# Six row buffers, earlier token numbers, zeros ahead of the first group, and ScalarE issuing the experts' weight loads in one layer of an eight-layer kernel

## The chip, the cores and the metric

One core of one Trainium2 chip runs one launch of the whole kernel. The metric is the device time of the launch in microseconds (us): the median of the runs shown.

## The reference, cut to what matters

The kernel computes eight residual blocks over 1024 tokens of 256 numbers. Only the fourth, called layer 3 in the kernel, is touched by the change. It is a mixture of experts: 128 experts are scored, 48 of them are kept, each token picks 8, and each expert takes at most 96 tokens.

```python
def _L1_ffn_ref(hidden_states, gate_weight, gate_up_proj, down_proj, old_to_new):
    NUM_EXPERTS = 128; NUM_KEPT = 48; TOP_K = 8; HIDDEN = 256; INTER = 96; CAP = 96
    logits = x @ gate_weight.T
    logits = jnp.where(old_to_new[None, :] == -1, -jnp.inf, logits)
    probs = jax.nn.softmax(logits, axis=-1)
    top_v, top_i = jax.lax.top_k(probs, TOP_K)
    top_v = top_v / jnp.sum(top_v, axis=-1, keepdims=True)
    sel_new = old_to_new[top_i]
    ...
    pos = jnp.sum(jnp.cumsum(oh, axis=0) * oh, axis=-1) - 1      # place of the token in its expert
    valid = pos < CAP
    xb = jnp.zeros((E, CAP + 1, H)).at[flat_e, pos_c].set(x[tok])[:, :CAP]
    gu = jnp.einsum('ech,eoh->eco', xb, gate_up_proj)
    g, u = jnp.split(gu, 2, axis=-1)
    out = jnp.einsum('eci,ehi->ech', jax.nn.silu(g) * u, down_proj)
    y = out[flat_e, jnp.minimum(pos_c, CAP - 1)]
    w = flat_w * valid
    final = jnp.zeros_like(x).at[tok].add(y * w[:, None])
```

## The kernel before

All matrix products split each float32 operand into a high and a low float16 part and sum three products (`mm3`, its matmuls carry line 863).

**Layer 3** takes the 48 experts in 12 groups of four (`QUADS`). The four experts of a group have 384 slots together, which are three chunks of 128 (`CHUNKS`). The work of group q is, engine by engine:

- **Slot numbers.** VectorE writes one-hot matrices (`one_hot`, L1982) that say which token sits in which slot. TensorE multiplies them with a table `wsplit` (`slots`, L1035) that holds each token's weights and, in its last 64 columns, its number (written at L1990). VectorE turns the result into indices (`slot_rows`, L1948 and L1949).
- **Rows.** GpSimd gathers the token rows of each chunk from the scratch table `rows` in HBM with an indirect DMA (L665) into one of `ROW_BUFS` = 4 buffers `x_rows`, all in the tile `sel`. SyncE's queue transposes each chunk into `xe[q % 2]` (`turn_rows`, L584). A gather into a used buffer waits for the transposes of the whole group that used it (L664). The transposes of a group wait until its three gathers have landed (L580) and those of the group before have landed (L582).
- **Weights.** SyncE's queue loads each expert's 320 KB into `w_in[:, j]` (`expert_load`, L569). ScalarE writes the high part (`weights_high`, L1561), VectorE the low part (`weights_low`, L1972). Groups 0 and 1 are loaded far ahead. From group 2 on an expert's load waits until VectorE is done with the buffer's last content (`we_lo`), and in the order of SyncE's queue the loads of group q + 3 stand behind the transposes of group q + 2.
- **Products.** TensorE: `gate_up(q)` (48 matmuls), `slots(q + 2)`, `combine(q - 1)` (48 matmuls of 256 columns into the accumulator, L1072), `down(q)` (L863 again). ScalarE: silu (L1573), high part of the hidden values (L1577), `weights_high(q + 1)`, and the high part of the group's three output chunks (L1587). VectorE: hidden values (L2009), `slot_rows(q + 2)`, low part (L2014), `slot_weights`, `weights_low(q + 1)`, `hot_turned(q)` (L1965), `one_hot(q + 3)`, and the low parts of the three output chunks (L2030).

The third output chunk's high part on ScalarE waits for VectorE's low part of the first. `slots(q + 2)`, which stands behind `gate_up(q + 1)` of the next turn, waits for all three low parts (L1118).

Ahead of group 0 stand, in a row on VectorE, `count_keys` (L1927, L1928, a wait for TensorE's sums, L1931), the token numbers (L1990), and the first `one_hot`. TensorE's queue has `slots(0)`, `turn_weights`, `slots(1)` and `map_weights` (L947, L948) before `gate_up(0)`.

`zeros16` is a tile of zeros; matmuls on it (L1115) clear an accumulator bank. `link` makes VectorE wait for its own last instruction.

Of the kernel before, what the change touches and what calls it, by code (L numbers as in the profile page):

```python
# [20 lines left out]
ALU = mybir.AluOpType  # L21
# [4 lines left out]
P = 128  # L26
D = 256
# [3 lines left out]
NT = T // P  # L31
# [28 lines left out]
KEPT = 48  # L60
# [4 lines left out]
QUAD = 4  # L65
QUADS = KEPT // QUAD
CHUNKS = QUAD * CAP // P
ROW_BUFS = 4
QS = QUAD * CAP
EW = 2 * 2 * INTER3 + D  # L70
# [56 lines left out]
def build(nc, w_blocks, w_experts, w_router, w_attn, x_in, ctxt, tok_ids, mask, g_all, l2_bias_rows, l2_bias_v,  # L127
          l4_gate, o2n_col, o2n_row, k_sel, k_rope, k_ident, k_ident16, k_tri, k_iota, k_slot, k_pick, k_token, k_tokens, out):
    ctx = ExitStack()
    with ctx:  # L130
# [7 lines left out]
        bank = [s2_all[:, i, :] for i in range(6)]  # L138
# [8 lines left out]
        xt_hi = sb("xt_hi", [P, KT, T], F16)  # L147
# [7 lines left out]
        w_in = sb("w_in", [P, RING, 3 * D])  # L155
# [137 lines left out]
        o = 8 * QS  # L293
        x_rows = [sel[:, o + n * 2 * D:o + (n + 1) * 2 * D] for n in range(ROW_BUFS)]
# [189 lines left out]
        def _(sp):  # L484
# [76 lines left out]
            def expert_load(e):  # L561
                j = e % QUAD
                if e >= 2 * QUAD:
                    sp.wait_ge(we_lo, e - 2 * QUAD + 1)
                elif e >= QUAD:
                    sp.wait_ge(we_first, j + 1)
                else:
                    sp.wait_ge(w_split, FFN[1][0] + FFN[1][1])
                sp.dma_start(w_in[:, j, 0:EW], w_experts[e]).then_inc(we_land[j], 16)  # L569
# [27 lines left out]
            for q in range(QUADS):  # L597
                for e in range(QUAD * (q + 2), min(QUAD * (q + 3), KEPT)):
                    expert_load(e)
                if q + 2 < QUADS:  # L600
                    turn_rows(q + 2)
# [255 lines left out]
        def _(pe):  # L857
# [163 lines left out]
            def experts3():  # L1021
# [81 lines left out]
                map_weights()  # L1103
                for q in range(QUADS):
# [357 lines left out]
        def _(act):  # L1462
# [91 lines left out]
            def experts3():  # L1554
# [9 lines left out]
                nc.scalar.activation(silu3[1][0:1, 0:1], ident[0:1, 0:1], ACT.Silu)  # L1564
                act.wait_ge(m_oldt, 3)
# [3 lines left out]
                for q in range(QUADS):  # L1569
# [10 lines left out]
                    for c in range(CHUNKS):  # L1580
# [4 lines left out]
                        if q > 1:  # L1585
                            act.wait_ge(s3_c, q - 1)
                        nc.scalar.activation(y16[q % 2][:, 0, c, :], bank[2 + c % 2][:, (c // 2) * D:(c // 2 + 1) * D],  # L1587
                                             ACT.Copy, scale=w_slot[:, q % 4, c:c + 1]).then_inc(s3_yh, 1)

# [189 lines left out]
        def _(dve):  # L1779
            n_own = [0]  # L1780

            def link(ins):

                n_own[0] += 1
                ins.then_inc(s_v, 1)
                dve.wait_ge(s_v, n_own[0])
# [136 lines left out]
            def count_keys():  # L1923
# [4 lines left out]
                link(nc.vector.tensor_scalar(one3, new, 1.0, None, ALU.min))  # L1928
                dve.wait_ge(m_cum, 1)
# [10 lines left out]
            def experts3():  # L1940
# [48 lines left out]
                for t in range(NT):  # L1989
                    m = nc.vector.tensor_scalar(wsplit[:, t, 2 * 64:3 * 64], zeros16[:, 0:64], token[:, 0:1], float(P * t),  # L1990
                                                ALU.add, ALU.add)
                link(m)
# [613 lines left out]
```

## Time and profile before

| | us |
|---|---|
| median of 3 runs | 1504.42 (1503.94 to 1505.86) |
| the profiled execution | 1502.56 |
| its span, first to last instruction | 1500.7 |
| TensorE busy | 1265.7 (84%) |
| VectorE busy | 1178.3 (79%) |
| GpSimd busy | 762.9 (51%) |
| ScalarE busy | 758.1 (51%) |
| mean granted clock of TensorE | 0.789 of full speed |

The span covers all eight layers; layer 3's part of it lies between about 684 and 871 us. Busy shares are averages over stages with different limits. The granted clock of TensorE is 1.00 (2.4 GHz) or 0.50 (1.2 GHz) at any moment.

### The profile page before, as it was taken

How to read it: one execution, taken by the hardware profiler on the slowest of the kernel's cores; microseconds unless marked ns; L12 is line 12 of the kernel's file. 1: busy time of each engine (PE TensorE's matmuls, PEld its weight loads, DVE VectorE, ACT ScalarE, POOL GpSimd, SP SyncE). 2: the span in 40 equal slices, each digit the busy share in tenths (PEclk: the TensorE clock that was granted, in tenths of full speed). 3: DMA queues.
4: the chain of work that ended last, by engine and by line, in shares of the span. 5: the costliest groups of instructions: out<-in, count | busy, mean ns of one | idle time of the engine just before them, and what ended most of it. 6: DMA issues, size and time to landing. Idle time of an engine off the chain costs nothing.

```text
span 1500.7 us, 30682 instructions
## 1 busy us (share of the span) xinstructions
PE 1265.7 (84%) x11448; PEld 778.8 (52%) x11448; DVE 1178.3 (79%) x2410; ACT 758.1 (51%) x1457; POOL 762.9 (51%) x727
## 2 busy tenths in 40 slices
PE   6878999999996999974798873888888889993798
PEld 3544555555553333233687761555555655562455
DVE  7858777777769999977787569888888767659784
ACT  4442222222236988863343334988999943331432
POOL 5444767676611005000332246988988947773262
PEclk9999999999997555557799995555555589996899
DMA  6120111111013999981556524998999921110010
GB/s 215 43 78 32 43 52 42 52 42 52 21 36 65 173 180 174 176 168 41 142 173 173 162 50 84 143 152 145 149 151 150 141 71 40 46 54 31 12 33 28
DMA packets 350670, 143.14 MB, mean 95 GB/s; under 512 B 328912, under 2 KB 331472, under 8 KB 349776
## 3 DMA queue, kind: packets, MB, share of 16 engines
q1 hardware_dynamic: 347232, 132.88, 42.7%
q0 software_dynamic: 1728, 4.72, 1.1%
q10 hardware_dynamic: 1584, 3.86, 0.8%
q8 instruction: 79, 1.29, 0.4%
q14 instruction: 47, 0.39, 0.1%
HBM read 59.09 MB, written 2.10 MB: 41 GB/s over the span
## 4 chain that ended last, share of the span: by engine, by line
PE 50%; DVE 27%; POOL 6%; ACT 5%; issue 5%; DMA 5%; SPq 1%; ACTq 0%; POOLq 0%; DVEq 0%
PE s_all L863 32%; DVE small L2250 7%; PE bank L863 6%; PE s_all L1072 2%; PE bank L1072 2%; POOL c_hi L772 2%; PE s_all L1254 2%; DVE stats L1791 1%; DVE small L2253 1%; POOL c_hi L770 1%; POOL c_lo L772 1%; PE s_all L977 1%; DVE ffbuf L2092 1%; PE bank L1389 1%; DVE xt_lo L1812 1%
## 5 line engine op out<-in xcount | busy, mean ns | idle before, releaser
L619 POOL TENSOR_TENSOR w_hi<-w_in,ws_col 128x768 f16<-128x768 f32 (+1 forms) x76 | 109.6, 1442 | 268.4 <-PE bank L863 259.5
L863 PE MATMUL s_all<-xt_hi,w_hi 128*128 128x512 f16 x576 | 172.5, 381 | 17.2 <-DVE ffbuf L2061 7.1
L2063 DVE TENSOR_TENSOR hid_lo<-ffbuf,hid_hi 128x512 f16<-128x512 f32 x80 | 142.2, 1778 | 56.4 <-ACT hid_hi L1501 56.4
L620 POOL TENSOR_SCALAR w_in<-w_in 128x768 f32<-128x768 f32 (+1 forms) x76 | 182.8, 2405 | 0.0
L1501 ACT ACTIVATE hid_hi<-ffbuf 128x512 f16<-128x512 f32 x80 | 50.4, 630 | 247.8 <-DVE ffbuf L2061 247.8
L863 PE MATMUL s_all<-xt_lo,w_hi 128*128 128x512 f16 x576 | 172.8, 382 | 0.0
L863 PE MATMUL s_all<-xt_hi,w_lo 128*128 128x512 f16 x576 | 172.4, 381 | 0.0
L1639 ACT ACTIVATE ag<-s_all,small 128x1024 int16<-128x1024 f32 x128 | 154.0, 1203 | 23.8 <-DVE small L2253 13.5
L2250 DVE TENSOR_REDUCE small<-s_all 128x1 f32<-128x1024 f32 x128 | 155.5, 1215 | 7.3 <-PE s_all L1254 7.2
L665 POOL DMA_INDIRECT sel<-rows,slot_misc x36 | 43.4, 1204 | 204.9 <-DVE slot_misc L1949 130.6
L1254 PE MATMUL s_all<-ag 32*128 32x512 f16 x256 | 131.5, 616 | 12.2 <-ACT ag L1639 7.4
L623 POOL TENSOR_TENSOR w_lo<-w_in,w_hi 128x768 f16<-128x768 f32 (+1 forms) x76 | 126.2, 1660 | 6.3
L1319 PE MATMUL s_all<-ag 32*128 32x256 f16 x512 | 91.6, 399 | 35.5 <-DVE small L2330 31.9
L1701 ACT ACTIVATE ag<-ffbuf,small 128x256 f32<-128x256 f32 x256 | 115.7, 507 | 0.2
L2098 DVE TENSOR_TENSOR hid_lo<-ffbuf,hid_hi 128x512 f16<-128x512 f32 x72 | 74.1, 1029 | 30.1 <-ACT hid_hi L1531 29.9
L1369 PE MATMUL s_all<-sel,ag 32*128 32x256 f16 x256 | 77.3, 403 | 24.2 <-DVE hid_lo L2361 6.6
L2330 DVE CUSTOM_DVE_ANT_0 ffbuf<-s_all,ffbuf 128x256 f32<-128x256 f32 x256 | 97.1, 416 | 0.0
L863 PE MATMUL s_all<-w_hi,hid_hi 128*128 128x256 f16 (+3 forms) x346 | 90.4, 276 | 3.4 <-DVE hid_lo L2098 3.4
L863 PEld LDWEIGHTS s_all<-xt_hi,w_lo 128*128 128x128 f16 x576 | 56.6, 98 | 69.0 <-issue 1.7
L863 PEld LDWEIGHTS s_all<-xt_lo,w_hi 128*128 128x128 f16 x576 | 56.4, 98 | 68.7 <-issue 1.1
L2092 DVE SCALAR_TENSOR_TENSOR ffbuf<-s_all,ffbuf 128x512 f32<-128x512 f32 x72 | 49.5, 688 | 51.8 <-ACT ffbuf L1524 51.6
L863 PE MATMUL s_all<-w_hi,hid_lo 128*128 128x256 f16 (+3 forms) x346 | 90.2, 275 | 0.0
(387 smaller groups left out, 3210.9 us busy)
## 6 DMA issues: line engine op xcount, KB each, us to landing
w_in<-in_w_blocks SPq DMA_DIRECT2D x76, 384.0 KB, 3.0
w_in<-in_w_experts SPq DMA_DIRECT2D x48, 320.0 KB, 4.8
region<-in_w_attn SPq DMA_DIRECT2D x4, 512.0 KB, 10.4
sel<-in_k_sel ACTq DMA_DIRECT2D x1, 1280.0 KB, 5.5
ag<-ag SPq DMA_TRANSPOSE x66, 3.4
x<-in_x_in SPq DMA_DIRECT2D x1, 1024.0 KB, 4.9
region<-in_ctxt SPq DMA_DIRECT2D x1, 1024.0 KB, 9.8
ffbuf<-in_mask ACTq DMA_DIRECT2D x1, 1024.0 KB, 5.4
```

The source lines that it names most:

```text
L619: nc.gpsimd.tensor_tensor(hi, w, ws_col[:, 0:1].broadcast_to([P, used]), ALU.mult).then_inc(s_g, 1)
L620: nc.gpsimd.tensor_scalar(w, w, WS, None, ALU.mult).then_inc(s_g, 1)
L623: nc.gpsimd.tensor_tensor(lo, w, hi, ALU.subtract).then_inc(w_split, 1)
L863: m = nc.tensor.matmul(outp, lhs, rhs, start=(first and n == 0), stop=(last and n == len(steps) - 1), skip_group_check=True)
L1254: m = nc.tensor.matmul(bank[2 * (n % S2_BUFS) + h][:, :], turned[s][0][r:r + 32, i * P:(i + 1) * P], turned[s][1][r:r + 32, h * HALF:(h + ...
L1319: return nc.tensor.matmul(bank[2 * (n % 2) + h][:, a_ * S:(a_ + 1) * S], q_t[r:r + 32, i * P:(i + 1) * P], (k_t, ak_t)[a_][r:r + 32, b * S ...
L1369: return nc.tensor.matmul(bank[4 + k % 2][:, kt * S:(kt + 1) * S], turned[s][2][r:r + 32, j * P:(j + 1) * P], q2_t[m % 2][r:r + 32, :], st ...
L1639: nc.scalar.activation(p2[n % P2_BUFS], s2[n % S2_BUFS], ACT.Exp, bias=small[:, 1, s * L2_UNITS + v:s * L2_UNITS + v + 1], scale=scale_g[s ...
L1701: m = nc.scalar.activation(p4[n % P4_BUFS][:, h, :], masked[:, n % 2, h, :], ACT.Exp, bias=small[:, 1, c:c + 1], scale=1.0)
L2063: nc.vector.tensor_tensor(hid_lo[:, h, :], hid[:, h, :], hid_hi[:, h, :], ALU.subtract).then_inc(s_hl, 1)
L2250: nc.vector.tensor_reduce(small[:, 0, c:c + 1], s2[(g * L2_UNITS + v) % S2_BUFS], AX.X, ALU.max).then_inc(G[2, "chain"], 1)
L2330: m = nc.vector.tensor_tensor_reduce(out=masked[:, n % 2, h, :], in0=bank[2 * (n % 2) + h][:, 0:S], in1=mask_sb[:, b, q, :], scale=1.0, sc ...
```

## The change

- `ROW_BUFS` goes from 4 to 6; the two new row buffers are pieces of `xt_hi`, the high part of layer 3's transposed input.
- The eight instructions that write the token numbers into `wsplit` move ahead of VectorE's wait for `m_cum`.
- Four matmuls of zeros with 512 columns are put ahead of `gate_up(0)`; they write bank 0.
- The loads of groups 2 to 11 leave SyncE's queue. ScalarE issues the four loads of group q + 2 in turn q, between the high parts of the second and the third output chunk, with the same waits on `we_lo`.

```diff
-ROW_BUFS = 4
+ROW_BUFS = 6
...
-        x_rows = [sel[:, o + n * 2 * D:o + (n + 1) * 2 * D] for n in range(ROW_BUFS)]
+        x_rows = [sel[:, o + n * 2 * D:o + (n + 1) * 2 * D] for n in range(4)] + \
+                 [xt_hi[:, 0, n * 2 * D:(n + 1) * 2 * D] for n in range(2)]
...
             def expert_load(e):
                 j = e % QUAD
-                if e >= 2 * QUAD:
-                    sp.wait_ge(we_lo, e - 2 * QUAD + 1)
-                elif e >= QUAD:
+                if e >= QUAD:
                     sp.wait_ge(we_first, j + 1)
...
             for q in range(QUADS):
-                for e in range(QUAD * (q + 2), min(QUAD * (q + 3), KEPT)):
-                    expert_load(e)
                 if q + 2 < QUADS:
                     turn_rows(q + 2)
...
                 map_weights()
+                for _ in range(4):
+                    nc.tensor.matmul(bank[0][:, :], zeros16[:, 0:P], zeros16[:, :], start=True, stop=True,
+                                     skip_group_check=True)
                 for q in range(QUADS):
...
+                def expert_loads(q):
+                    for e in range(QUAD * q, QUAD * (q + 1)):
+                        act.wait_ge(we_lo, e - 2 * QUAD + 1)
+                        act.dma_start(w_in[:, e % QUAD, 0:EW], w_experts[e]).then_inc(we_land[e % QUAD], 16)
+
...
                         nc.scalar.activation(y16[q % 2][:, 0, c, :], bank[2 + c % 2][:, (c // 2) * D:(c // 2 + 1) * D],
                                              ACT.Copy, scale=w_slot[:, q % 4, c:c + 1]).then_inc(s3_yh, 1)
+                        if c == 1 and q + 2 < QUADS:
+                            expert_loads(q + 2)
...
                 link(nc.vector.tensor_scalar(one3, new, 1.0, None, ALU.min))
+                for t in range(NT):
+                    m = nc.vector.tensor_scalar(wsplit[:, t, 2 * 64:3 * 64], zeros16[:, 0:64], token[:, 0:1], float(P * t),
+                                                ALU.add, ALU.add)
+                link(m)
                 dve.wait_ge(m_cum, 1)
...
-                for t in range(NT):
-                    m = nc.vector.tensor_scalar(wsplit[:, t, 2 * 64:3 * 64], zeros16[:, 0:64], token[:, 0:1], float(P * t),
-                                                ALU.add, ALU.add)
-                link(m)
                 one_hot(0)
```

## Rows read from the trace of the kernel before

**Rows 1.** Stretch of groups 2 to 10: length, busy PE, PEld, DVE, ACT, POOL, clock, DMA
```profile
747.58:850.95 103.37, 91.03 (x1247) 80.01 (x1246) 77.61 (x185) 44.82 (x84) 33.00 (x31) 0.95 0.60 177
```

**Rows 2.** Waits in layer 3 (TensorE from 747.5 to 863.7): total, times, longest
```profile
PE s_all L863 <- issue: 11.1, 7, 2.5
...
ACT region L1561 <- DMA w_in<-in_w_experts: 0.3, 1, 0.3
...
POOL sel L665 <- DMA sel<-sel: 40.0, 11, 4.8
...
SPq L582 <- DMA sel<-rows,slot_misc: 57.3, 10, 6.8
```

**Rows 3.** Timeline of GpSimd, two turns: start, length, what, idle before
```profile
769.59 0.94 POOL L665 DMA_INDIRECT sel<-rows,slot_misc  x1 [3.59 <-DMA sel<-sel]
770.84 0.95 POOL L665 DMA_INDIRECT sel<-rows,slot_misc  x1 [0.30 <-issue]
...
780.25 2.53 POOL L665 DMA_INDIRECT sel<-rows,slot_misc  x1 [3.61 <-DMA sel<-sel]
```

**Rows 4.** Timeline of SyncE's queue, the turn before
```profile
764.14 3.82 SPq L584 DMA_TRANSPOSE sel<-sel  x3
768.00 2.21 SPq L569 DMA_DIRECT2D w_in<-in_w_experts  x4
```

**Rows 5.** DMAs by tile, median us to landing; last, min/median/max for L569
```profile
sel<-rows,slot_misc POOLq DMA_INDIRECT x36, 4.0
sel<-sel SPq DMA_TRANSPOSE x36, 2.6
...
DMA to landing us min/median/max: 3.9/4.8/6.0
```

**Rows 6.** Timeline of VectorE: low parts of the third output chunk, and one turn
```profile
748.97 0.48 DVE L2030 SCALAR_TENSOR_TENSOR ffbuf<-s_all,slot_misc,ffbuf 128x256 f16<-128x256 f32 x1 [0.23 <-ACT ffbuf L1587]
...
783.46 0.55 DVE L2009 SCALAR_TENSOR_TENSOR ffbuf<-s_all,ffbuf 96x384 f32<-96x384 f32 x1
...
785.35 3.02 DVE L1972 SCALAR_TENSOR_TENSOR w_lo<-w_in,w_hi 128x640 f16<-128x640 f32 x4
...
792.64 0.48 DVE L2030 SCALAR_TENSOR_TENSOR ffbuf<-s_all,slot_misc,ffbuf 128x256 f16<-128x256 f32 x1 [0.29 <-ACT ffbuf L1587]
...
839.76 0.48 DVE L2030 SCALAR_TENSOR_TENSOR ffbuf<-s_all,slot_misc,ffbuf 128x256 f16<-128x256 f32 x1 [0.29 <-ACT ffbuf L1587]
862.95 0.48 DVE L2030 SCALAR_TENSOR_TENSOR ffbuf<-s_all,slot_misc,ffbuf 128x256 f16<-128x256 f32 x1 [0.29 <-ACT ffbuf L1587]
```

**Rows 7.** Chain of waits: start, length, what (one turn, and the start of layer 3)
```profile
706.06 1.27 DVE wsplit L1990 x8
723.26 4.09 PE s_all L863 x48
...
792.28 2.33 PE s_all L863 x48
794.61 0.58 PE s_all L1035 x24
...
800.45 1.55 PE s_all L863 x21
802.00 2.52 issue
```

**Rows 8.** Timeline: VectorE's wait for the sums, TensorE's zeros
```profile
705.06 0.96 DVE L1931 SCALAR_TENSOR_TENSOR cwt<-s_all,ag 128x768 f16<-128x768 f32 x1 [1.32 <-PE s_all L929]
...
723.26 0.56 PE L863 MATMUL s_all<-sel,w_hi 128*96 128x96 f16 x4 [1.81 <-DMA sel<-sel]
...
728.46 1.01 PE L1115 MATMUL s_all<-zeros 128*128 128x512 f16 x2
```

**Rows 9.** DMAs that ScalarE issues just before layer 3
```profile
684.72 0.45 ACTq L1747 DMA_DIRECT2D cwt<-in_k_slot  x1
685.20 0.46 ACTq L1748 DMA_DIRECT2D slot_misc<-in_k_pick  x1
```

## The prediction

> **What bounds the kernel now.** I read layer 3 from the outside in. The busy time of the stretch of groups 2 to 10 [rows 1] shows no engine full: of 103.37 us TensorE is busy for 91.03, VectorE for 77.61, and DMA for 0.60. The list of waits [rows 2] says what the others are for. TensorE stands 11.1 us, in 7 waits, before a `gate_up` that "waits for nothing that the profile shows". GpSimd stands 40.0 us in 11 waits for the transposes, and SyncE's queue 57.3 us for the gathered rows. That is a ring: gathers wait for transposes, transposes for gathers.
>
> The timelines close it. The transposes of group 4 are issued from 764.14 to 767.96 [rows 4], and 2.6 us is the median from issue to landing [rows 5]. At 769.59 GpSimd resumes, with a wait that ended on the transposes [rows 3]. It issues the second gather of group 5, at 770.84 the third; these land about 4.0 later [rows 5], group 5's transposes follow, and at 780.25 the second gather of group 6 is let go [rows 3]. So with four buffers two of three gathers of each group stand behind the whole transposition of the group before, and the ring needed 10.7 us in this turn. TensorE follows: its `gate_up(6)` and `gate_up(7)` start at 792.28 and, after an unexplained 2.52, at 804.52 [rows 7], 12.2 apart.
>
> As the beat I take the end of the third low piece on VectorE, which lets the next turn's `slots` go. It ends at 748.97 + 0.48 = 749.45 for group 1, at 840.24 for group 9 and at 863.43 for group 11 [rows 6]. Eight turns take 90.8, **11.35 a turn**, and the last two 23.2.
>
> **What each engine would need without the ring.** VectorE's turn from 783.46 to 793.12, in which it never waited long, is 9.66 [rows 6]. TensorE's is `gate_up` 2.33, `slots` 0.58, `combine` 5.26 (795.19 to 800.45) and `down` 1.55 [rows 7], 9.72.
>
> **The change part by part.**
>
> *Six buffers.* A gather then waits for the transposes of two groups back, so the path of a group becomes: numbers, three gathers of 0.95 with 0.30 between [rows 3], third landing 4.0 after its issue, three transposes (the third issued 2.55 after the first), 2.6 to land: 2.5 + 4.0 + 2.55 + 2.6 = 11.65. With a gather of 2.53 as at 780.25, and 6.0 to land for the rows, some 15.2. The numbers come in turn q, just after `slots(q + 2)`, and `gate_up(q + 2)` begins 17.4 later at a turn of 10.9 (two turns less 4.4 from the beginning of `gate_up` to the first gather: 2.33, a wait of 0.7, `slots`, two VectorE instructions and 0.4 of start). The ring falls off the path by 2 to 6 us. The two buffers lie in `xt_hi`, which layer 3's router has long read, and no wait is added for them. The gathers now overlap other VectorE work, which is covered by the same margin.
>
> *Loads on ScalarE's queue.* This part has a price. SyncE is rid of four issues, 2.21 in [rows 4], which were worth nothing there, since its queue waits for rows anyway [rows 2]. ScalarE pays for them between its second and third output piece, and behind them wait the third high piece, VectorE's third low piece, the next silu, and TensorE's `slots`. ScalarE's own issues come 0.48 apart [rows 9], so four cost 1.95. Let `down` end at 0. The second high piece is dispatched at once, the issues end at 2.0, the third high piece (0.48) at 2.5, the low piece (0.48) at 3.05. Before, that third piece waited only for VectorE's first low piece. From there: `slots` to 3.7, `combine` to 9.0, `down` to 10.55. `gate_up` (2.33) is hidden in it. So the turn is **10.55**, TensorE and ScalarE in one ring, 0.9 over VectorE's need.
>
> The trace first, then the rule: these rows show issue time on either queue to be alike, 0.45 to 0.5. The Trainium skill, "DMA: Bandwidth & Descriptors", section "Issuing engines are not separate DMA queues", says that all issuing engines feed the same 16 DMA engines and that a second one only saves the sequencer's issue time. By that rule the move adds no bandwidth, and the rows agree that SyncE's issue time bought nothing; by it alone one would leave the loads where they are.
>
> *When the loads land.* Now they are issued from 0.05 to 1.5 after `down`, beside the transposes of the same group, no longer behind them. ScalarE's high parts could begin at about 4.15 (silu, hidden values, their high part). A load lands 4.8 after issue, 3.9 to 6.0 [rows 5]; VectorE has to begin its low parts by 6.0 or so for the turn of 10.55 (they begin at 785.35 and the third low piece ends 7.77 later, 0.29 of it a wait [rows 6]: 7.5, and 3.05 + 10.55 - 7.5 is 6.1). First load 4.85 plus 0.65 for its high part: 5.5, in time. At 6.0 to land it is 0.7 late. The transposes beside it speak for more than the median, so I add 0.35 a turn: **10.9**. Ends: 10.0 (issues cheaper than the row) and 11.7 (loads 1.2 late).
>
> *Token numbers sooner.* They cost 1.27 on the chain [rows 7]; in front of the wait for the sums VectorE is idle for 1.32 [rows 8]. So they fit, and everything after moves by 1.25. If that idle time were not there they would cost the same as before: bounds 0 and 1.3.
>
> *Zeros in front.* Before `gate_up(0)` TensorE waits 1.81 for the transposes [rows 8]. Two such matmuls at half clock take 1.01 and overlap, so four take 1.7: hidden, 0.1 or 0.2 late at worst. What they can bring is the clock: `gate_up(0)` took 4.09 at 0.50 where the same 48 matmuls take 2.33 at 1.00 [rows 7], so 1.76 is the upper end. The engine had been busy for the whole 4.09 without the clock rising. I take 0.5, bounds -0.2 and 1.8.
>
> **The sum.** Group 1's beat: 749.45 - 1.25 - 0.5 = 747.7. Groups 2 to 9, the last with loads behind them: 8 x 10.9 = 87.2, to 834.9. Group 10 has no issues, but its weights come late as before: 10.2, to 845.1. Group 11 has no `slots` and no wait for rows: `gate_up` 2.33, `combine` 5.26, `down` 1.55 less what overlaps the group before, 9.4 in all, to 854.5. Against 863.43 that is 8.9 saved. What follows is a chain of dependent layers and keeps it. The profiled execution was 1502.56, 1.86 below the median, so 1493.7 there and **1495.5 for the median**.
>
> **The rivals.**
>
> *The loads become the bound (0.13).* For it: DMA is at 0.60 of the stretch already [rows 1], and transposes and loads now coincide. At 11.7 a turn, 11.0 for group 10: 747.7 + 93.6 + 11.0 + 9.4 = 861.7, 1.7 saved, 1502.7. Against: ScalarE waited for these loads once in the trace before, for 0.3 [rows 2].
>
> *The change doesn't free the ring (0.05).* If the rows are still last, for instance because each gather is blocked by VectorE as the one at 780.25 was, only the start is gained: 1.75, again 1502.7.
>
> *ScalarE's issues are held up by SyncE's (0.08), the slower side.* In the new order the transposes are issued about when ScalarE issues its loads. If one generator serves both, ScalarE waits for up to 3.82 [rows 4] in every turn, and the third piece with it: 14.4 a turn, 747.7 + 115.2 + 10.2 + 9.4 = 882.5, 19.1 lost, 1523.5. It decides from a turn of 12.0, that is when four issues take 3.4 instead of 1.95. For it: the trace has no issue of ScalarE beside one of SyncE. Against: SyncE's loads, issued while its transposes were under way, still took 0.55 each [rows 4].
>
> *The issues cost next to nothing (0.08).* Then VectorE and TensorE bound the turn at about 10.0: 747.7 + 80 + 9.7 + 9.4 = 846.8, 16.6 saved, 1487.8. ScalarE's issues in the trace ran beside its own activations. The Trainium skill, the same page, section "Anatomy of one DMA", puts the sequencer's dispatch at about 50 ns, so four would be 0.2 and this case the likeliest. The 0.48 of [rows 9] decides against it.
>
> **How the numbers follow.** My case has 0.66. The range 1490.5 to 1503.5 takes turns from 10.3 to 11.7 with the bounds of the start, leaving out the slower rival and the cheapest case. About 0.2% (3 us) is what a measurement can tell from no change. Faster by more: my case nearly whole, the cheap case, and a part of the late loads: 0.79. Same: 0.12. Slower: 0.09.
>
> **What would show it.** Right: GpSimd's wait for the transposes near 0 instead of 40.0; TensorE's unexplained waits before `gate_up` gone, a wait of some 0.7 before `slots` for VectorE's third low piece instead; four issues of 0.48 on ScalarE's queue per turn; beats 10.5 to 11.3 apart; the numbers' 1.27 inside the former idle 1.32. Wrong: gathers still released by transposes; issues on ScalarE over 0.8 each; waits of ScalarE's high parts for the loads above 1.5 a turn; beats of 11.7 or more.

## The result and the profile after

The changed kernel takes 1511.01 us in the median of 17 runs (1506.70 to 1515.84). The kernel before, in 17 runs beside it, takes 1505.83 (1499.45 to 1511.85). The ratio is 1.0039, 95% interval [1.0025, 1.0053]: the change costs about 6 us where 9 were forecast to be saved, and lies outside the range. The profiled execution took 1511.56 with a span of 1509.7; the mean granted clock, 0.79, is as before. Of the runs further down, one of e8 (1867.44 us) and one of the kernel before beside e9 to e12 (5885.69 us) were slow ones, and the ratios leave them out.

As in the prediction, the beat is the end of the third low piece on VectorE. VectorE's timeline of the changed kernel, for groups 1, 9 and 11 (start, length, what, idle before):

```profile
748.88 0.48 DVE L2037 SCALAR_TENSOR_TENSOR ffbuf<-s_all,slot_misc,ffbuf 128x256 f16<-128x256 f32 x1 [1.66 <-ACT ffbuf L1592]
...
849.17 0.48 DVE L2037 SCALAR_TENSOR_TENSOR ffbuf<-s_all,slot_misc,ffbuf 128x256 f16<-128x256 f32 x1 [0.71 <-ACT ffbuf L1592]
...
868.29 0.48 DVE L2037 SCALAR_TENSOR_TENSOR ffbuf<-s_all,slot_misc,ffbuf 128x256 f16<-128x256 f32 x1 [0.29 <-ACT ffbuf L1592]
```

Group 1 ends at 749.36, group 9 at 849.65, group 11 at 868.77. Eight turns take 100.29, **12.54 a turn**, where [rows 6] gave 11.35 and the prediction 10.9. Group 11 is 5.34 later than before, as much as the medians differ. (The two profiled executions lie 9.0 apart; the rest of that comes after group 11, mostly in later layers, which the change doesn't touch.)

The waits of layer 3 in the changed kernel (total, times, longest):

```profile
ACT region L1561 <- DMA w_in<-in_w_experts: 14.2, 10, 2.4
PE s_all L1032 <- DVE ffbuf L2037: 14.2, 9, 2.3
ACT ffbuf L1592 <- issue: 5.8, 3, 2.4
ACT w_hi L1561 <- DMA w_in<-in_w_experts: 4.7, 5, 1.4
POOL sel L662 <- DMA sel<-xt_hi: 0.3, 1, 0.3
```

Set beside [rows 2]: GpSimd's 40.0 us behind the transposes have gone to almost nothing, so the ring is free. TensorE's unexplained 11.1 us before `gate_up` are gone too. In their place TensorE waits 14.2 us in front of `slots` for VectorE's third low piece, 1.6 a turn where the prediction expected 0.7, and ScalarE, which waited 0.3 us for loads, waits 14.2 + 4.7 = 18.9.

The chain of waits says the same: between 745 and 862 a third of it, 32.6%, is loads on their way. The page lists the landing (issues on ScalarE's queue, KB each, median us to landing; the line of L1568 gives the minimum and maximum, as [rows 5] does):

```profile
771.71 8.65 DMA w_in<-in_w_experts
...
799.11 6.44 DMA w_in<-in_w_experts
822.26 7.63 DMA w_in<-in_w_experts
```

```profile
w_in<-in_w_experts ACTq DMA_DIRECT2D x40, 320.0 KB, 5.3
...
DMA to landing us min/median/max: 2.9/5.3/8.8
```

A load now takes up to 8.8 us where it took 3.9 to 6.0. One turn on ScalarE shows what that does:

```profile
770.82 0.37 ACTq L1568 DMA_DIRECT2D w_in<-in_w_experts  x1
770.86 0.47 ACT L1592 ACTIVATE ffbuf<-s_all,slot_misc 128x256 f16<-128x256 f32 x1
771.23 1.66 ACTq L1568 DMA_DIRECT2D w_in<-in_w_experts  x3
773.07 0.47 ACT L1592 ACTIVATE ffbuf<-s_all,slot_misc 128x256 f16<-128x256 f32 x1 [1.75 <-issue]
...
777.93 0.74 ACT L1561 ACTIVATE region<-w_in 128x640 f16<-128x640 f32 x1 [2.23 <-DMA w_in<-in_w_experts]
780.38 1.50 ACT L1561 ACTIVATE region<-w_in 128x640 f16<-128x640 f32 x2 [1.71 <-DMA w_in<-in_w_experts]
```

The four issues hold the third piece for 1.75 us, about as forecast. The first high part begins at 774.99, and the other three were to follow it without a gap. But the second waits 2.23 us for its load, and the last two another 1.71.

There is a third thing, which the prediction does not have. The same stretch turn by turn (length, busy PE, PEld, DVE, ACT, POOL, granted clock, DMA share, GB/s):

```profile
749.36:761.69 12.33, 9.90 (x141) 8.61 (x141) 9.07 (x24) 5.05 (x9) 2.97 (x3) 1.00 0.79 194
761.69:774.06 12.37, 11.32 (x141) 9.34 (x141) 9.02 (x24) 4.83 (x9) 3.43 (x3) 0.86 0.70 155
774.06:787.48 13.42, 9.90 (x141) 8.61 (x141) 9.06 (x24) 4.94 (x9) 2.97 (x3) 1.00 0.91 190
787.48:800.72 13.24, 11.52 (x141) 9.47 (x141) 8.96 (x24) 4.83 (x9) 3.77 (x3) 0.87 0.74 141
```

The granted clock is 1.00 in one turn and 0.86 or 0.87 in the next. In the turns at 0.86 and 0.87 TensorE needs 11.4 us for the 141 instructions that take 9.90 in the others. TensorE's timeline at the start of such a turn shows where:

```profile
761.75 0.78 PE L1032 MATMUL s_all<-wsplit,ag 128*128 128x6 f16 x24 [2.34 <-DVE ffbuf L2037]
762.39 1.87 PE L1069 MATMUL s_all<-ffbuf,ag 128*128 128x256 f16 x8
764.05 1.68 PE L1069 MATMUL bank<-ffbuf,ag 128*128 128x256 f16 x8
765.57 1.04 PE L1069 MATMUL s_all<-ffbuf,ag 128*128 128x256 f16 x8
```

The engine stood for 2.34 us, and then some 16 matmuls of `combine` ran at 1.2 GHz before the clock was back at 2.4 (eight of them take 1.87 and 1.68 us there, and 1.04 afterwards). These slow matmuls are on the chain:

```profile
762.53 1.73 PE s_all L1069 x8
764.26 1.47 PE bank L1069 x8
765.73 0.87 PE s_all L1069 x8
```

The length of the wait alone does not decide it. Of the eight turns four are at 0.86 or 0.87; three of them stand behind waits of 2.34, the fourth behind one of 1.35, while a turn behind a wait of 1.71 is at 1.00. In e14 below, a turn behind a wait of 2.34 is at 1.00 too:

```profile
783.09 0.76 PE L1034 MATMUL s_all<-wsplit,ag 128*128 128x6 f16 x24 [2.34 <-DVE ffbuf L2039]
```

### The profile page after: what moved, and what is told of

It reads as the page before. It is cut to its first block, busy times and chain, and to the rows that moved or that the text cites. A ratio compares the mean times of both kernels' runs of the same rounds, so it can differ in the third digit from the quotient of the medians.

```text
span 1509.7 us, 30690 instructions
## 1 busy us (share of the span) xinstructions
PE 1269.9 (84%) x11452; PEld 777.7 (52%) x11452; DVE 1184.5 (78%) x2410; ACT 758.8 (50%) x1457; POOL 760.5 (50%) x727
## 4 chain that ended last, share of the span: by engine, by line
PE 45%; DVE 28%; DMA 7%; POOL 7%; ACT 6%; issue 4%; SPq 1%; ACTq 1%; POOLq 0%; DVEq 0%
PE s_all L860 30%; DVE small L2257 7%; PE bank L860 6%; DMA w_in<-in_w_experts 3%; POOL c_hi L769 2%; POOL c_lo L769 2%; PE s_all L1254 2%; PE s_all L1069 2%; DVE stats L1798 1%; DVE small L2260 1%; POOL c_hi L767 1%; PE bank L1069 1%; PE s_all L974 1%; DVE ffbuf L2099 1%; DMA sel<-c_lo 1%
## 5 line engine op out<-in xcount | busy, mean ns | idle before, releaser
L662 POOL DMA_INDIRECT sel<-rows,slot_misc x24 | 25.9, 1080 | 204.7 <-DVE slot_misc L1960 201.1
## 6 DMA issues: line engine op xcount, KB each, us to landing
region<-in_w_attn SPq DMA_DIRECT2D x4, 512.0 KB, 10.2
```

## Which part of the change costs

Four kernels take the change apart. Each stands beside runs of the kernel before on its own chip; differences between kernels that ran on different chips are therefore taken from the ratios, 0.001 being 1.5 us. The intervals of the ratios reach 2 to 4 us to either side, so such a difference is good to a few us only. Where a kernel and the changed kernel are compared by turns, it is one profiled execution of each.

**e1_loads_on_sync.** The changed kernel with the loads of groups 2 to 11 back where they were:

```diff
-                        if c == 1 and q + 2 < QUADS:
-                            expert_loads(q + 2)
...
+                if e >= 2 * QUAD:
+                    sp.wait_ge(we_lo, e - 2 * QUAD + 1)
...
+                for e in range(QUAD * (q + 2), min(QUAD * (q + 3), KEPT)):
+                    expert_load(e)
```

> The changed kernel with the loads of groups 2 to 11 back in SyncE's queue, in their old place ahead of the group's transposes; six buffers, token numbers and zeros stay. Theory (T1): the loss comes from the loads on ScalarE's queue, which were issued beside the transposes and landed up to 8.8 us later, after the point where VectorE needs them. Then here the loads are issued as soon as VectorE has left the buffer, some 2 to 3 us before the transposes, the beat of the loop falls to about 9.7 to 10.5 us and the kernel takes 1490 to 1497, faster than before by 0.5 to 1%. Rival (T2): the six buffers themselves cost (gathers and transposes now collide with loads whoever issues them). Then this one stays at 1507 to 1512.

Measured: 1492.88 us, ratio 0.9925 [0.9900, 0.9949]. So the move of the loads makes the changed kernel 17 us slower than it is with them on SyncE. SyncE's queue, two turns:

```profile
770.09 2.56 SPq L585 DMA_TRANSPOSE sel<-xt_hi  x2
772.69 2.03 SPq L570 DMA_DIRECT2D w_in<-in_w_experts  x4
777.59 4.44 SPq L585 DMA_TRANSPOSE sel<-sel  x3
782.07 2.03 SPq L570 DMA_DIRECT2D w_in<-in_w_experts  x4
```

With six buffers SyncE is free as soon as VectorE has read the old weights. The loads go out at 772.69, behind one group's transposes and 4.9 us ahead of the next group's, and land in 4.4 us in the median, 6.5 at most. ScalarE never waits for one. The turns, by VectorE's beats, with the clock at 1.00 throughout:

```profile
758.59:768.27 9.68, 9.62 (x140) 8.50 (x141) 8.99 (x22) 4.34 (x8) 3.88 (x3) 1.00 0.73 210
768.27:778.73 10.46, 9.92 (x147) 8.67 (x144) 8.89 (x22) 5.31 (x10) 3.43 (x3) 1.00 0.71 212
```

**e2_scalar_loads_alone.** The kernel before with the loads on ScalarE's queue and nothing else (four buffers; no numbers or zeros moved).

> The kernel before with the loads of groups 2 to 11 on ScalarE's queue and nothing else. T1 (the move of the loads is what costs): slower than before by 3 to 10 us, beats of 12 us or more, ScalarE's high parts waiting for loads. T2 (the move is harmless without six buffers): within 2 us of before.

Measured: 1511.78 us, 1.0039 [1.0016, 1.0063]. Alone, the move costs as much as the whole change, but by another way: ScalarE waits only 2.8 + 1.9 us for loads, and the chain goes through TensorE's waits before `gate_up`, 14.9 us (5.0 at the longest) where they were 11.1. GpSimd waits 40.4 us for the transposes, as before; a transpose takes up to 8.1 us to land where it took 4.7. With four buffers the rows are last, and the loads beside them make them later.

**e3_six_buffers_alone.** The kernel before with `ROW_BUFS = 6` and the two buffers in `xt_hi`.

> The kernel before with six row buffers and nothing else, loads on SyncE. T1: 6 to 11 us faster than before, GpSimd's wait for the transposes gone, beats 9.7 to 10.5. T2: no faster than before.

Measured: 1493.86 us, 0.9938 [0.9915, 0.9961]. The six buffers alone are worth about 9 us; turns of 9.67 and 10.47 follow each other as in e1.

**e4_scalar_loads_earlier.** The changed kernel with the four issues right behind `weights_high(q + 1)` instead of between two output pieces, so before `combine` has ended:

```diff
+                    if q + 2 < QUADS:
+                        expert_loads(q + 2)
...
-                        if c == 1 and q + 2 < QUADS:
-                            expert_loads(q + 2)
```

> The changed kernel, with ScalarE's four issues moved from between the second and third output piece to right behind the high parts of the weights, where ScalarE waits for TensorE anyway; still ScalarE's queue. If only the place in ScalarE's order matters (late issue, and the third output piece behind it), the loads land 2 to 3 us sooner relative to their use and it takes 1493 to 1499. If ScalarE's queue beside SyncE's transposes is itself the trouble, it stays above 1504, with loads still taking 7 us or more to land.

Measured: 1498.81 us, 0.9957 [0.9936, 0.9977]. Now no engine waits for a load, and still it is 5 us behind e1, which issues at nearly the same moment from SyncE. The chain has waits before `gate_up`, which are for the transposed rows:

```profile
767.59 2.16 issue
...
791.39 3.23 issue
```

The waits end as the transposes of groups 4 and 6 land. By the landings in the trace, the last transpose of these groups takes 6.6 and 7.6 us from issue to landing, and 2.7 and 3.2 in e1. The gathers before them are later by less: the third takes 5.7 and 5.4 us, and 5.3 and 4.6 in e1. Here ScalarE issues the next group's loads about when SyncE issues these transposes (762.71 to 764.92, beside 759.88 to 763.10); in e1 they stand behind the transposes in one queue. The loads are ahead, the rows pay.

## What the move costs, in its parts

**e5_issues_behind_third.** The condition of the issues goes from `c == 1` to `c == 2`.

> The changed kernel with ScalarE's four load issues moved from behind the second to behind the third output piece of the group. Theory P (the third output piece, held 1.7 to 2.4 us behind four issues, is what the change costs): the third piece follows its low piece at once, the turn falls from 12.4 us to about 10.9, and the time to some 1495 us. Theory L (the loads come too late, the third piece is not what decides): the third piece is sooner, but the loads are issued about 0.9 us later, ScalarE waits longer for them (L1561 for w_in, 14.2 us in the changed kernel, grows to about 20), and the time stays at 1511 or rises to some 1515 us.

Measured: 1513.97 us, 1.0079 [1.0052, 1.0107]. The third piece is sooner, but then the next silu stands behind the issues, 16.0 us in 9 waits. The loads are issued later and land sooner after it (median 3.9 us, at most 6.8), and ScalarE waits 8.4 + 4.8 us for them, less than the 18.9 before, not more. Still the loads are 40.3% of the chain from 745 to 862, and the clock is at 0.85 to 0.88 in five of the eight turns. So neither theory fits as it was written: not P, for the time did not fall, and not L, for the waits for loads did not grow.

**e6_sync_loads_late.** e1 with one more wait for each load, so that SyncE issues at the moment at which ScalarE does in the changed kernel:

```diff
+                    sp.wait_ge(s3_y, CHUNKS * (e // QUAD - 1))
                     sp.wait_ge(we_lo, e - 2 * QUAD + 1)
```

> The changed kernel with the loads on SyncE's queue, as in e1_loads_on_sync (1492.88 us), but each group's loads held there until down of the group two before has ended, the moment at which ScalarE issues them in the changed kernel. Theory late (it is the moment of the issue that costs, on whatever queue): loads reach w_in too late as in the changed kernel, ScalarE waits some 10 to 14 us for them, and the time is 1505 to 1511 us. Theory queue (the second queue beside the transposes makes each load slow): with one queue the loads land in 4.5 us, ScalarE waits for them little, and the time stays within 3 us of 1493 to 1496.

Measured: 1499.01 us, 0.9967 [0.9953, 0.9980]. Between both theories: 0.0042 or 6 us over e1 for lateness. ScalarE waits 5.7 + 1.1 us for loads. Two things come with the lateness and are in the 6 us: the clock falls here too in two turns (0.85), and on SyncE's queue the transposes stand behind the late loads.

**e9_hold_alone.** e1 with ScalarE held by spare copies where the issues would be. From the start of the second piece to that of the third it is 2.0 us here (some 766.65 to 768.66), and 2.2 in the changed kernel (770.86 to 773.07), so the copies stand in for the issues a little short:

```diff
+                        if c == 1 and q + 2 < QUADS:
+                            for spare in (xt_hi, xt_lo):
+                                for c0 in (0, 384):
+                                    nc.scalar.activation(spare[:, 1, c0:c0 + 384], zeros16[:, 0:384], ACT.Copy)
```

> The kernel of e1_loads_on_sync (loads on SyncE's queue in the old place, 1492.88 us) with ScalarE held between its second and third output piece by four spare copies (128x384, some 0.5 us each, 2.0 in all) in the turns in which the changed kernel issues loads there: the price of the place of the issues alone, with loads neither late nor on a second queue. Theory turn (as in the prediction: the held third piece makes the turn 10.55 where it was 10.05 in e1_loads_on_sync): 9 or 10 turns of 0.5 to 0.9 more, 1497 to 1502 us. Rival (the hold falls into time that ScalarE and TensorE have, since loads and rows are early): within 2 us of 1493.

Measured: 1497.02 us, 0.9958 [0.9945, 0.9971]: 0.0033 or 5 us more than e1, with intervals that just overlap. Its turns are the plainest of all:

```profile
758.95:769.65 10.70, 9.86 (x141) 8.59 (x141) 8.87 (x23) 6.24 (x13) 3.77 (x3) 1.00 0.68 199
769.65:780.35 10.70, 9.86 (x141) 8.61 (x141) 8.86 (x24) 6.25 (x13) 3.77 (x3) 1.00 0.67 199
```

Seven turns from 748.24 to 823.17 take 10.70 each. The prediction worked out 10.55 for exactly this ring: `down`, the held third piece, `slots`, `combine`, `down`.

**e10_late_and_hold.** e6 and e9 in one. Against the changed kernel the second queue is missing, and with it the overlap of loads and transposes.

> The same with both: loads on SyncE's queue held until down of the group two before has ended, as in e6_sync_loads_late (1499.01 us), and ScalarE held for 2.0 us. Only the second queue is missing against the changed kernel (1511.01 us). Theory queue (loads on a queue of their own beside the transposes land late, and that is most of the cost): 1500 to 1504 us, and the 7 to 11 us up to the changed kernel belong to the second queue. Rival (late issue and held piece together make it all): 1508 to 1511 us.

Measured: 1501.26 us, 0.9982 [0.9968, 0.9996]. Lateness and hold together cost 0.0057 over e1, 9 us, and what is left to the changed kernel, the second queue and 0.2 us a turn of longer hold, is another 0.0057, again 9. Issued in the same moment, a load lands in 3.4 us (2.9 to 5.9) on SyncE's queue here, in 4.4 (2.8 to 7.4) in e6, and in 5.3 (2.9 to 8.8) on ScalarE's. On one queue the transposes come behind the loads; on two they run together. This pair of runs can't part the queue from the running together; e8 and e15 below, where loads on ScalarE's queue land in 4.4 and 4.0 us once the transposes are held or halved, speak for the latter.

**e7_half_loads.** The changed kernel whose loads from group 2 on carry 320 of 640 columns, so the products use old weights in the rest:

```diff
-                        act.dma_start(w_in[:, e % QUAD, 0:EW], w_experts[e]).then_inc(we_land[e % QUAD], 16)
+                        act.dma_start(w_in[:, e % QUAD, 0:EW // 2], w_experts[e][:, 0:EW // 2]).then_inc(we_land[e % QUAD], 16)
```

> The changed kernel with ScalarE's loads of groups 2 to 11 carrying only the first 320 of 640 columns (the other half of each buffer keeps older weights): the same number of issues in the same places, half the bytes. Theory P (the third piece behind the issues decides): the issues cost the same, the turn stays near 12.4 us, 1508 to 1511 us. Theory L (the landing of the loads decides): they land in 3 to 3.5 us instead of 5.3, ScalarE's waits for w_in vanish, the turn is 10.5 to 10.9 as the prediction had it with loads in time, and the time falls to 1494 to 1497 us.

Measured: 1504.46 us, 1.0006 [0.9986, 1.0026]. The loads land in 3.1 us and ScalarE's waits for them drop from 18.9 to 3.1, as theory L says; the time gains only 5 us of the 15 it expected. The windows tell why, with turns of 11.2 at full clock and of 12.7 and 12.9 at 0.87 (behind waits of only 1.38 and 1.35 us). And the issues are now 15.0% of the chain from 748 to 845.

**e8_transposes_held.** The changed kernel, each group's transposes held until its loads are there:

```diff
+                    sp.wait_ge(we_land[QUAD - 1], 16 * (q + 3))
                     turn_rows(q + 2)
```

> The changed kernel with each group's transposes on SyncE held until the group's four loads (on ScalarE's queue) have landed; nothing else moves. Theory contention (the loads land late because they share the DMA engines with the transposes issued in the same moment from the other queue): the loads land in 4.0 to 4.8 us with a maximum near 6, ScalarE's waits for w_in fall from 14.2 to below 6 us, and the time falls to 1499 to 1504 us, unless the rows now come late for gate_up. Theory late (without contention the loads would be too late all the same): the landing improves by less than 0.5 us, and the time stays within 3 us of 1511.

Measured: 1506.24 us, 1.0004 [0.9983, 1.0026]. The wait for the loads and the turns:

```profile
ACT region L1562 <- DMA w_in<-in_w_experts: 1.8, 4, 0.8
```

```profile
751.65:762.27 10.62, 9.48 (x136) 8.32 (x137) 9.01 (x23) 4.56 (x8) 4.00 (x3) 1.00 0.69 202
762.27:773.07 10.80, 9.93 (x150) 8.75 (x148) 8.90 (x23) 4.83 (x9) 3.43 (x3) 1.00 0.68 192
773.07:784.00 10.93, 7.63 (x98) 6.44 (x95) 8.99 (x23) 4.94 (x9) 3.43 (x3) 1.00 0.65 187
784.00:798.86 14.86, 13.51 (x189) 12.29 (x189) 8.89 (x24) 5.20 (x10) 3.43 (x3) 0.89 0.52 149
```

Without transposes beside them the loads are nearly in time (4.4 us, 6.8 at most), and three turns are the 10.6 to 10.9 of the prediction. But in them the rows fall behind, until TensorE waits 3.39 us for them and a turn takes 14.86. Over eight turns the mean is 12.53 (751.65 to 851.90), no better than in the changed kernel, and the time is above the 1499 to 1504 of the one theory and below the other's 1508. That is the bargain in which the changed kernel stands: loads and transposes want the same few microseconds.

**e11_zeros_before_slots.** The changed kernel with TensorE kept at work in front of `slots`. The zeros are added to the sums, which they leave as they are:

```diff
+                        if q < QUADS - 1:
+                            for b in (4, 5, 6, 7, 4, 5):
+                                nc.tensor.matmul(bank[b][:, :], zeros16[:, 0:P], zeros16[:, :], start=False,
+                                                 stop=False, skip_group_check=True)
                         pe.wait_ge(s3_yl, CHUNKS * q)
```

> The changed kernel with six matmuls of zeros (128x512, added to the sums, 1.3 us at full clock) on TensorE between gate_up and the wait in front of slots, groups 1 to 10. In the changed kernel the granted clock is 1.00 and 0.86 in turns, and in the latter 16 to 24 matmuls of combine take 1.87 and 1.7 instead of 0.87 per eight. Theory clock (TensorE's idle time before slots lets its clock fall, and the slow combine costs up to 1.7 us every second turn): all turns at 1.00, 4 to 7 us less, 1504 to 1507 us. Rival (the loads decide the turn anyhow, the slow combine falls into time that TensorE has): the clock stays at 1.00 but the time is within 2 us of 1511, or later by what the zeros hold up.

Measured: 1501.52 us, 0.9982 [0.9968, 0.9997]. Two turns of it:

```profile
749.64:760.69 11.05, 11.05 (x149) 9.05 (x147) 9.14 (x24) 5.05 (x9) 2.96 (x3) 1.00 0.92 191
760.69:773.89 13.20, 11.25 (x148) 9.05 (x147) 9.13 (x23) 4.94 (x9) 3.17 (x3) 1.00 1.02 199
```

The clock stays at 1.00 in all eight turns, and 0.0057, some 9 us, come back although the loads are nearly as late as before (ScalarE waits 9.5 + 5.8 us, and the longest landing is 9.3). Between the two profiled executions group 11's beat is 6.0 earlier. More useless work makes this kernel faster. The shares overlap, of course: late loads and held pieces are what makes TensorE stand.

**e13_half_loads_zeros, e14_half_transposes, e15_half_transposes_zeros.** The first is e7 with e11's zeros (and old weights in half of each buffer, as there). The second transposes only the high half of each chunk's rows from group 2 on, so the low half of the input is an old one; the third is that with the zeros. The edit of e14:

```diff
-                    sp.dma_start(xe[q % 2][:, :, :, c * P:(c + 1) * P].rearrange("p a k s -> p (a k) s"),
-                                 x_rows[(q * CHUNKS + c) % ROW_BUFS], transpose=True).then_inc(s3_xe, 16)
+                    a = slice(0, 2) if q < 2 else slice(0, 1)
+                    sp.dma_start(xe[q % 2][:, a, :, c * P:(c + 1) * P].rearrange("p a k s -> p (a k) s"),
+                                 x_rows[(q * CHUNKS + c) % ROW_BUFS][:, 0:(2 if q < 2 else 1) * D], transpose=True
+                                 ).then_inc(s3_xe, 16)
```

> e7_half_loads (320 of 640 columns loaded on ScalarE's queue from group 2 on) and e11_zeros_before_slots in one: nothing late and the clock kept, with the issues where the change has them. Theory sum (the late landing and the fallen clock are all that parts the changed kernel from the prediction): the turn is the 10.70 us of e9_hold_alone, and the time 1495 to 1498 us. Rival (something else costs too): over 1499 us, turns over 11.

> The changed kernel with SyncE's transposes of groups 2 to 11 carrying only the high half of each chunk's rows (128x256 instead of 128x512; the low half keeps older values), the loads whole. Theory contention (the transposes beside them make the loads late): the loads' landing falls from a median of 5.3 and a maximum of 8.8 us to about 4.5 and 7, ScalarE's waits for them from 18.9 us to below 9, the clock is kept in more turns, and the time is 1499 to 1504 us. Rival (a load on ScalarE's queue is slow by itself): the landing changes by less than 0.3 us and the time stays within 3 us of 1511.

> e14_half_transposes with the zeros of e11_zeros_before_slots: the clock is kept, so that what is left against e13_half_loads_zeros is lateness of the loads alone. Theory contention: loads nearly in time, turns of 10.7 to 11.2, 1496 to 1500 us, below e11_zeros_before_slots (1501.52 us). Rival: no faster than that, 1501 to 1503 us.

Measured: e13 1499.41 us, 0.9954 [0.9938, 0.9971]; e14 1504.59, 1.0000 [0.9982, 1.0017]; e15 1498.22, 0.9946 [0.9932, 0.9961]. In e14 the loads' longest landing falls from 8.8 to 7.3 us and the waits from 18.9 to 11.0, but the median stays at 5.3, where about 4.5 was expected; in e15 it is 4.0 and 5.4 at most. Against e11, with the clock kept in both, half the transposes take the landing from 5.0 us (9.3 at most) to 4.0 (5.4) and 0.0036, 5 us, off the time. Together with the zeros they take 0.0093, 14 us, off the changed kernel, to within 2 us of the prediction. But in both the turn is about 11.2 (seven turns from 751.08 to 829.28 in e13, from 751.00 to 829.69 in e15), not 10.70: here the rival was right. What is left shows in e13 as ScalarE standing 12.0 us in 6 waits behind its own issues: the four take 1.9 to 2.7 us there, 2.2 in the mean, where the copies of e9 held it for 1.65. That is about the 0.5 us a turn; by itself it was not tried.

**e12_start_alone.** The kernel before with only the token numbers and the four zeros moved.

> The kernel before with only the two small parts of the change: the token numbers in front of the wait for the sums, and four matmuls of zeros in front of gate_up(0). By the prediction's terms (1.25 and 0.5): 1.75 us less than before, ratio 0.9988. Rival (what the numbers gain is lost in the landing of the first transposes, and in the first turns the ring of buffers swallows it): within 0.5 us of before, ratio 0.9997 to 1.0003.

Measured: 1503.10 us, 0.9991 [0.9979, 1.0003]: 1.4 us less, near the prediction's 1.75, but not told from nothing. The start of layer 3 in the changed kernel, from its chain:

```profile
703.35 1.27 DVE wsplit L1937 x8
704.65 0.97 DVE cwt L1942
...
718.13 3.87 DMA sel<-sel
721.99 0.04 issue
722.04 3.39 PE s_all L860 x48
```

**e16_loads_on_sync_again and e17_constants_later.** In the kernels with six buffers and loads early on SyncE's queue the turn of group 9 is about 2 us longer than its fellows (12.07 in e1, 12.16 in e3, and 12.35 in e9, where the others are 10.70). The three instructions that the two expectations call additions are `hot_turned`'s comparisons (`tensor_scalar` with `is_equal`). e16 is e1 once more, and e17 is e1 with

```diff
                 pool.wait_ge(s3_w, 1)
+                pool.wait_ge(s3_hot_t, CHUNKS * (QUADS - 2))
                 for a_ in range(2):
                     nc.gpsimd.memset(v9[:, a_, :, :].rearrange("p t (h c) -> p (t h) c", c=VC)[:, :, ones:VC], VS * (1 - a_))
```

> The kernel of e1_loads_on_sync once more, to stand beside e17_constants_later on the same chip: 1491 to 1495 us, ratio 0.991 to 0.994, turns of 9.7 to 10.5 with one of about 12.1 for group 9, in which three additions of VectorE (L1973) take 5.4 instead of 1.27 us while GpSimd writes its constants.

> The same with GpSimd's five fills for attention 4, which follow its last gather, held until VectorE has made hot_turned of group 9. Theory collision (the fills beside VectorE's f16 additions are what makes them 5.4 us long): the three additions take 1.27 us, group 9's turn is 10.5 or less instead of 12.1, and the time is 1.5 us below e16_loads_on_sync_again, 0.1% in the ratio. Rival (the additions are slow for another reason, or the fills slow VectorE's next instructions as much): group 9's and group 10's turns together stay within 0.3 us of what they were.

Measured: e16 1493.01 us, 0.9922 [0.9894, 0.9950]; e17 1490.06, 0.9903 [0.9880, 0.9926]. The intervals overlap, so the times don't show a gain; the turns do. VectorE in e16, and GpSimd in e16 beside it:

```profile
822.69 5.79 DVE L1973 TENSOR_SCALAR ag<-ag,slot_misc 128x1024 f16<-128x1024 f16 x3
```

```profile
823.60 1.25 POOL L797 MEMSET v<- 128x256 f16 x1
...
827.26 0.56 POOL L799 MEMSET av_w<- 128x64 f32 x1
```

and VectorE in e17:

```profile
824.42 1.27 DVE L1974 TENSOR_SCALAR ag<-ag,slot_misc 128x1024 f16<-128x1024 f16 x3
```

Group 9's turn falls from 12.20 to 10.12, group 10's goes from 8.89 to 9.08. e17 has the lowest ratio of the study, about 1% below the kernel before.

## Why the prediction was wrong

**The ring: right.** Group by group the gathers no longer wait for transposes, and six buffers alone save 9 us. The second rival (the ring not freed) is out.

**The issues: nearly right.** They were to take 1.95 a turn; they take 1.8 to 2.7, 2.1 in the mean over eight turns. One issue takes 0.44 in the median and 0.33 to 0.78, but for a single one of 1.34. The ring behind them was given as 10.55 and measures 10.70. The third rival's mechanism, issues held up by SyncE's, did not come about, though its side did. The fourth rival is out as well. The Trainium skill's figure from "DMA: Bandwidth & Descriptors", section "Anatomy of one DMA — SWDGE (gpsimd) path", some 50 ns for a dispatch, does not price these rows; the section is about transfers that GpSimd issues, and these are ScalarE's.

**"So I add 0.35 a turn": this is the step that failed.** It stood for the landing of the loads beside the transposes. The prediction took the median of 4.8, let the first load be "in time" with 0.5 to spare, and took the 6.0 of [rows 5] as the worst. But those rows were measured with the loads behind the transposes on one queue. Beside them a load takes 5.3 in the median and up to 8.8, and on the chain stand the third and the last of the four, not the first (the 8.65 from 771.71 is the third). ScalarE waits 18.9 us for them in all, and the turn is 12.54. With nearly the same hold and the loads early on SyncE's queue it is 10.70 (e9). The prediction's own signs of being wrong came: waits for loads above 1.5 a turn, and beats of 11.7 or more. The rival "loads become the bound" named the mechanism and had 0.13, but took its price from the same rows, 1.2 us, and so ended at 11.7 a turn.

The rule weighed there, "Issuing engines are not separate DMA queues", in "DMA: Bandwidth & Descriptors" of the Trainium skill, says that a second queue saves issue time only. The traces agree in the sign: the saved issue time bought nothing. What the rule does not say, and e10 against the changed kernel shows, is that loads on a second queue, running together with the transposes, cost up to 9 us here.

**The clock: a missing term.** The prediction foresaw that TensorE would wait before `slots`, 0.7 us a turn, and gave that wait no price beyond its length. At 0.85 a turn, as in e9, it would have had none: from group 2 to group 9 all turns there are at 1.00. At 1.35 and 2.34 the clock fell in four of the eight turns. The sum has matmuls of `combine` at 5.26 in every turn, and in half of them the turn's matmuls take 1.3 to 1.6 us more. By e11 this is worth up to 9 us; as the loads come in the way of both, the two shares can't be added.

**Group 9: a term that was missing, and cost nothing here.** GpSimd's fills fall into the turn of group 9 instead of group 10 and meet VectorE's comparisons, in the changed kernel too:

```profile
842.29 5.38 DVE L1976 TENSOR_SCALAR ag<-ag,slot_misc 128x1024 f16<-128x1024 f16 x3
```

But they are not on its chain, which goes through the slow `combine` and ScalarE's issues there, and group 9's turn, 12.67, is no longer than the other turns at 0.87. In e9, which has the ring of the prediction without the late loads, the same meeting made the turn 12.35 instead of 10.70. So a kernel in which the loads had come as forecast would have been some 1.7 us over the sum by this. In the kernel before the fills ran from 842.31 to 846.54, next to VectorE's low parts.

**The sum.** Predicted: 747.7 + 87.2 + 10.2 + 9.4 = 854.5. Measured: 749.36 + 100.29 + 10.24 + 8.88 = 868.77. Of the 14.3 between them 13.1 lie in the eight turns and 1.7 at the start. There the numbers did move as described: their 1.27 ends at 704.62 and `cwt` follows at 704.65 with no wait for the sums between, so they just fill the idle time. `gate_up(0)` begins at 722.04 instead of 723.26 and takes 3.39 instead of 4.09, so the zeros gave 0.7 where 0.5 was forecast. Group 0 ends at 735.63 against 737.50, 1.87 sooner where 1.75 was forecast: this part was right. But group 1 loses it again, in a turn of 13.73 that already has ScalarE's issues in it. It is 13.57 in e9 with the copies in their place, and 12.30 in e1 with neither.

**What the fee hid.** The 8.9 us forecast were there to be had: e3 had about 9 by the row buffers alone, and e1 about 11. What was wrong was to treat the loads as a small fee. With them left on SyncE the same kernel takes 1493, a little less than was forecast.

## What to carry to other kernels

Freeing a ring moves the idle time of a queue, so ask again where each transfer then runs: here SyncE, once free of waiting, issued the loads in a gap of its own, and moving them away put them in the busiest moment. A landing time taken from a trace holds only for what ran beside it; price the last of a group of transfers, beside its new neighbours. And a wait given to TensorE in a loop may cost twice, once as idle time and once as a slower clock behind it; here waits of 1.35 to 2.34 us did so in some turns and not in others.

## What the runs showed of the hardware

- In some turns TensorE's granted clock was at 0.50 for about 3 us of `combine` behind a wait before `slots`. In the changed kernel these waits were 2.34 (three times) and 1.35 us, in e7 1.38 and 1.35. It stayed at 1.00 behind one of 1.71 in the changed kernel and one of 2.34 in e14, and behind all those of up to 0.85 in e1 and e9 from group 2 on. Six matmuls of zeros in the wait kept it at 1.00 in all turns of e11.
- Three f16 comparisons of VectorE (128x1024, with one tensor read) took 5.4 to 5.8 us instead of 1.27 beside GpSimd's fills. The f32 instructions with two tensors beside the same fills in the kernel before, or in e17, took their usual time. The Trainium skill, "SBUF — State Buffer", section "Who interferes with whom", says that VectorE in its two-port modes and GpSimd lock each other out of a shared port pair for whole instructions, and counts `tensor_scalar` among the candidates. The traces fit; no run here varied the mode itself.
- Loads of 320 KB, issued in the same moment, landed in 3.4 or 4.4 us in the median (e10, e6) on the transposes' own queue, ahead of them, and in 5.3 on another, beside them. On the other queue it was 4.4 with the transposes held (e8), and 4.0 with them halved and the zeros in (e15).
